# A DLRM tower on one core: ten features by one-hot matmul, two samples per dot-product matmul, gathers issued two at a time

## The chip, the core and the metric

The kernel runs on one core of a Trainium2 chip. The metric is the device time of one execution in microseconds (us). The engines are named as the profile names them: PE (TensorE, matmuls), PEld (its weight loads), DVE (VectorE), ACT (ScalarE), POOL (GpSimd, which issues the gathers), SP (SyncE, which issues the other transfers).

## The reference

2048 samples. Each has a dense vector of 128 numbers and 26 ids, each of which picks one row of 128 numbers from its own table. The tables have 1000, 1250, 12500 or 125000 rows.

```python
e = jnp.stack([tbl_0[ids[:, 0]], ..., tbl_25[ids[:, 25]]], axis=1)
combined = jnp.concatenate([dense_features[:, None, :], e], axis=1)        # 27 vectors of 128
interactions = jnp.einsum('bnd,bmd->bnm', combined, combined)
z = jnp.concatenate([dense_features, interactions[:, _TRIU_I, _TRIU_J]], axis=1)   # 351 pairs
h = jnp.concatenate([z, r_dense_features], axis=1)
h = jnp.maximum(h @ W_top1 + b_top1, 0.0)     # 607 -> 512
h = jnp.maximum(h @ W_top2 + b_top2, 0.0)     # 512 -> 256
y = h @ W_top3                                # 256 -> 1
```

## The kernel before

The batch is 16 tiles of 128 samples; a step handles two tiles (256 samples), so there are 8 steps, and the steady ones run in a hardware loop with two steps per iteration. Vector 0 is the dense one, vectors 1 to 26 the features.

**Fetching a feature.** The vectors come in two ways.
- Nineteen features per tile are gathered: POOL issues an indirect DMA for each (L322 in `gather_tile`), which brings 128 rows of 512 bytes, one per sample, into `rows[v % 2]`. The features are in five groups (3, 4, 4, 4 and 4 gathers; the first group also holds the dense vector). Ahead of group k of tile v POOL waits until PE has transposed group k of tile v-2, which frees that part of the buffer (L317). Nothing else holds a gather back, so POOL issues up to 19 in a row. PE then turns each vector with a transpose (L359) into `vec_ps`, and ACT and DVE by turns copy groups into `vecs` (L577).
- Seven features (`SPREAD`, all with tables of 1000 rows) are fetched by one-hot matmuls, called items. The table lies in SBUF as 125 partitions by 8 rows, split into `t_hi` and `t_lo`. PE copies a feature's ids onto all partitions (L388, `ids_ps`), DVE compares them with the row numbers in two halves (L726, `onehot`), PE multiplies (16 matmuls of 256 columns, L406, into `fetch_ps`), and ACT copies the result into `vecs` (L594). The items of a step fetch for the next step. There is one `fetch_ps`, so an item waits for the ACT copy of the one before.

**Dot products.** One matmul per sample (L381): the sample's 27 vectors against themselves, 128 per tile, in four quadrants of 32 samples. ACT copies the 27x27 products into `inter` (L630, 16 copies per tile), DVE merges those of a second place over them (L805, 16 per tile); then ACT and DVE split `inter` into `x_hi` and `x_lo` (L638, L815).

**Layers.** Layer 1 (L453, 60 matmuls of 256 columns per step), layer 2 (L469), layer 3 (L483), with the activations on ACT (L650, L656). They run for the step before the one being fetched.

**Order.** The order on PE, ACT and DVE is written by hand in each engine's `step`; PE's mixes items and layers between transposes and dot products, so that a tile's transposes come once per half step. POOL's order is plain: tile after tile, group after group. The tables for the items are loaded by SP at the start (seven of 512 KB), together with the weights.

## Time and profile of the kernel before

| | us |
|---|---|
| median of 3 runs | 721.52 (720.75 to 726.87) |
| span of the profiled execution | 724.9 |
| PE busy | 437.8 (60%) |
| PEld busy | 397.8 (55%) |
| POOL busy | 294.0 (41%) |
| DVE busy | 276.1 (38%) |
| ACT busy | 195.9 (27%) |
| moved by DMA | 28.01 MB, mean 39 GB/s |

The profiled execution is one of its own, 3.4 us above the median. Busy time is that in which an engine executes; what ended the idle time ahead of an instruction is called its releaser and is inferred from semaphores. "issue" means that nothing the profile shows was waited for; "remote" that the releaser was not found. Matmuls overlap in the pipeline, so the distance between their starts, not their own length, is what a row of them costs.

### The profile page before, as it was taken

Reading aid. Unit: us, or ns where it says so; the run is one execution under the profiler, and the core shown is the slowest. Engines: PE = TensorE matmul, PEld = TensorE weight load, DVE = VectorE, ACT = ScalarE, POOL = GpSimd, SP = SyncE. Lnnn points to the kernel's source line nnn. Section 1 sums busy time; section 2 is a strip of 40 time slices with the busy share of each in tenths; the row PEclk is TensorE's granted clock in tenths of the full one; section 3 lists DMA queues with packets and bytes.
Section 4 is the critical chain, followed back from the end, with each engine's and each line's share of the span. In section 5 each row is a group of like instructions: output and inputs, shape, how many; then the busy total and the mean of one; then the engine's idle time right before and its main releaser. Section 6 shows DMA issues by size and latency. Waiting matters only on the chain.

```text
span 724.9 us, 14518 instructions
## 1 busy us (share of the span) xinstructions
PE 437.8 (60%) x6057; PEld 397.8 (55%) x6057; DVE 276.1 (38%) x465; ACT 195.9 (27%) x443; POOL 294.0 (41%) x314
## 2 busy tenths in 40 slices
PE   4206365482955839276491856829376494946987
PEld 2206355471944729265391845728375383835886
DVE  4506444350523616234152433425134351532450
ACT  1104132140511314132240413204132141412552
POOL 7761716336072542706336072541706336171000
PEclk9957776697886959679596786959779596876999
DMA  5531211102020110201102020110201101020000
GB/s 128 166 107 37 52 60 45 30 23 52 2 57 18 32 44 15 56 7 42 34 22 53 3 55 20 37 37 12 55 12 45 29 21 48 13 58 13 3 2 1
DMA packets 19576, 28.01 MB, mean 39 GB/s; under 512 B 10691, under 2 KB 13267, under 8 KB 19518
## 3 DMA queue, kind: packets, MB, share of 16 engines
q0 software_dynamic: 9728, 19.94, 10.9%
q1 hardware_dynamic: 9790, 7.17, 3.4%
q8 instruction: 52, 0.85, 0.5%
q14 instruction: 6, 0.05, 0.0%
HBM read 27.08 MB, written 0.01 MB: 37 GB/s over the span
## 4 chain that ended last, share of the span: by engine, by line
PE 44%; another core or an unknown queue 27%; issue 16%; ACT 7%; DVE 3%; DMA 2%; SPq 1%; ACTq 0%; DVEq 0%
PE dots_ps L381 18%; PE fetch_ps L406 12%; PE h_ps L453 4%; PE vec_ps L359 4%; PE h_ps L469 3%; DMA vecs<-in_tbl 2%; ACT vecs L577 2%; ACT vecs L594 2%; DVE inter L805 2%; ACT inter L630 1%; PE ids_ps L388 1%; PE fetch_ps L453 1%; DVE vecs L577 1%; DVE onehot L726 1%
## 5 line engine op out<-in xcount | busy, mean ns | idle before, releaser
L322 POOL DMA_INDIRECT rows<-in_tbl,idx x304 | 291.5, 959 | 360.3 <-PE vec_ps L359 264.5
L406 PE MATMUL fetch_ps<-onehot,t_hi 125*128 125x256 f32 x448 | 134.5, 325 | 130.1 <-ACT vecs L594 108.3
L381 PE MATMUL dots_ps<-vecs 128*27 128x27 f32 x4096 | 136.0, 197 | 89.1 <-issue 56.8
L381 PEld LDWEIGHTS dots_ps<-vecs 128*27 128x27 f32 x4096 | 130.7, 114 | 98.9 <-issue 98.2
L726 DVE TENSOR_TENSOR onehot<-ids_ps,row_of 125x1024 fp32r<-125x1024 f32 x94 | 111.4, 1220 | 176.0 <-remote 134.7
L406 PEld LDWEIGHTS fetch_ps<-onehot,t_hi 125*128 125x128 f32 x448 | 97.8, 218 | 136.4 <-issue 129.2
L406 PE MATMUL fetch_ps<-onehot,t_lo 125*128 125x256 f32 x448 | 131.1, 321 | 7.6 <-issue 7.6
L406 PEld LDWEIGHTS fetch_ps<-onehot,t_lo 125*128 125x128 f32 x448 | 97.7, 218 | 11.5 <-issue 7.9
L805 DVE COPY_PREDICATED inter<-mask,dots_ps 27x128 f32<-27x128 int32 (+2 forms) x256 | 66.9, 261 | 97.1 <-ACT inter L630 90.8
L594 ACT COPY vecs<-fetch_ps 128x256 f32<-128x256 f32 x56 | 37.7, 673 | 223.4 <-remote 153.8
L630 ACT COPY inter<-dots_ps 27x128 f32<-27x128 f32 (+1 forms) x256 | 64.1, 250 | 74.3 <-PE dots_ps L381 65.4
L577 ACT COPY vecs<-vec_ps 128x512 f32<-128x512 f32 x40 | 48.0, 1199 | 103.4 <-remote 57.2
L577 DVE COPY vecs<-vec_ps 128x512 f32<-128x512 f32 x40 | 47.3, 1181 | 61.5 <-remote 50.8
L359 PE MATMUL vec_ps<-ident,rows 128*128 128x128 f32 x320 | 47.4, 280 | 6.3 <-ACT vecs L577 4.4
L359 PEld LDWEIGHTS vec_ps<-ident,rows 128*128 128x128 f32 x320 | 37.2, 143 | 11.2 <-issue 6.1
L453 PE MATMUL h_ps<-x_hi,w_hi 128*128 128x256 f32 x140 | 37.1, 296 | 0.5 <-ACT x_hi L638 0.5
L453 PE MATMUL h_ps<-x_hi,w_lo 128*128 128x256 f32 x140 | 36.3, 290 | 0.0
L726 DVE TENSOR_TENSOR onehot<-h_ps,row_of 125x1024 fp32r<-125x1024 f32 x16 | 19.5, 1227 | 42.9 <-remote 37.7
L483 PE MATMUL h_ps<-w_sb,h_sb 128*128 128x1 f32 x48 | 11.2, 355 | 39.0 <-ACT h_sb L656 20.6
L483 PEld LDWEIGHTS h_ps<-w_sb,h_sb 128*128 128x128 f32 x48 | 10.7, 327 | 40.2 <-ACT h_sb L656 21.3
L469 PE MATMUL h_ps<-h_sb,w_sb 128*128 128x256 f32 x128 | 32.5, 381 | 0.1
L453 PEld LDWEIGHTS h_ps<-x_hi,w_hi 128*128 128x128 f32 x140 | 26.6, 190 | 1.3 <-issue 0.7
(65 smaller groups left out, 232.5 us busy)
## 6 DMA issues: line engine op xcount, KB each, us to landing
rows<-in_tbl,idx POOLq DMA_INDIRECT x304
vecs<-in_tbl SPq DMA_DIRECT2D x6, 500.0 KB
rows<-in_r_dense_features SPq DMA_DIRECT2D x16, 64.0 KB
h_sb<-in_W_top_laid SPq DMA_DIRECT2D x2, 512.0 KB
w_sb<-in_W_top SPq DMA_DIRECT2D x1, 512.0 KB
w_sb<-in_tbl SPq DMA_DIRECT2D x1, 500.0 KB
idx<-in_ids SPq DMA_DIRECT2D x16, 13.0 KB
w_dense<-in_W_top SPq DMA_DIRECT2D x1, 256.0 KB
```

Of the source, the lines that this page charges most:

```text
L322: nc.gpsimd.indirect_dma_start(out=rows[v % 2][:, s, :], out_offset=None, in_=tables[f - 1][:, :], in_offset=bass.IndirectOffsetOnAxis(ap= ...
L359: last = pe.transpose(vec_ps[kk % 2][:, n * P:(n + 1) * P], rows[u][:, s, :], ident[:])
L381: last = pe.matmul(dots_ps[q * 32:q * 32 + N, n // HALF, o:o + N], vs[:, b, :], vs[:, b, :], start=True, stop=True)
L406: last = pe.matmul(fetch_ps[:, 0:R], part[0:KP, k, h * KH + t, :], onehot[buf][h][0:KP, t, :], start=(h == 0 and t == 0 and part is t_hi), ...
L453: last = pe.matmul(bank[:, m, :], w[:, jj, c0:c0 + P], x[:, jj, :], start=(at == 0), stop=(at == 3 * (JG + 1) - 1))
L469: last = pe.matmul(h2_ps[:, m, :], w2_sb[:, k, m * P:(m + 1) * P], h1_sb[:, k, :], start=(n % M1 == 0), stop=(n % M1 == M1 - 1))
L483: last = pe.matmul(y[:, t:t + 1], h2_sb[:, k, t * P:(t + 1) * P], w3_sb[:, k:k + 1], start=(k == 0), stop=(k == M2 - 1))
L577: copy(vecs[v // 2][:, v % 2, :, a:a + n].rearrange("p b f -> p f b"), vec_ps[kk % 2][:, 0:n * P].rearrange("p (f b) -> p f b", f=n)).then ...
L594: nc.scalar.copy(vecs[slot][:, :, :, NR + k], fetch_ps[:, 0:R].rearrange("p (t b) -> p t b", t=2)).then_inc(fetched, 1)
L630: nc.scalar.copy(inter_of(q, g, 0, count[g]), products_of(q, g * JG, count[g])).then_inc(inter_by_act, 1)
L726: dve.tensor_tensor(onehot[buf][h][0:KP], ids_at(m)[0:KP].rearrange("p (o r) -> p o r", o=1).to_broadcast([KP, KH, R]), row_of[0:KP, h * K ...
L805: dve.copy_predicated(inter_of(q, g, a, n), mask[g * 32:g * 32 + N, a:a + n].rearrange("p (j h s) -> p j h s", h=1, s=1).to_broadcast([N, ...
```

## The change

- Three more features (2 and 8, tables of 1250 rows, and 1, of 1000 rows) are fetched by items: ten items per step instead of seven. An item of a 1250-row table has 20 matmuls and compares ten rows per partition instead of eight. Sixteen features per tile are gathered, in groups of 2, 4, 4, 4 and 2.
- All gathers go out by two: before each pair POOL waits until the pair ahead of it has landed (`gathered`). Ahead of a tile's first pair it also waits until the whole of tile v-2 is transposed, where before each group had a wait of its own. The first pass over four tiles is written out ahead of the loop.
- Dot products: one matmul handles two neighbouring samples. Its stationary operand is 64 columns (2 samples of 27 vectors padded to 32), its moving one 54; the products of a sample with itself are two diagonal blocks of the result. `dots_ps` holds 64 samples, so a tile is two units with 32 matmuls each, and a unit waits until the one before is copied and merged. There are 32 product copies and 32 merges per tile, each of half the samples.
- An item's result goes to `found` by one contiguous copy, and `place` puts all ten into `vecs` with one copy per tile (128x128x10). `vecs` holds one step instead of two.
- The ids of the item features come transposed from memory; PE turns none. Each table is loaded in two transfers (112 and 13 partitions), 2 of 640 KB and 8 of 512 KB in all. Layer 1 runs as four parts in two banks (`mlp_ps`), layer 3 with the weights stationary, the result is written as rows. The orders of PE, ACT and DVE are written anew. The memory set aside for POOL's DMA descriptors is set to 2048.

The diff, cut:

```diff
-SPREAD = (5, 6, 9, 14, 18, 24, 26)
+SPREAD = (2, 8, 1, 5, 6, 9, 14, 18, 24, 26)
+AT_ONCE = 2
...
-    groups = [list(range(a, min(a + 4, NR))) for a in range(0, NR, 4)]
+    groups = [list(range(a, b)) for a, b in ((0, 3), (3, 7), (7, 11), (11, 15), (15, 17))]
...
+    KT = [tables[f - 1].shape[0] // KP for f in SPREAD]
...
-        vecs = [sb(f"vecs{s}", [P, 2, P, N]) for s in range(2)]
+        vecs = sb("vecs", [P, 2, P, NP])
+        found = sb("found", [P, X, R])
...
-        dots_ps = ps("dots_ps", [P, 2, 512])
+        dots_ps = ps("dots_ps", [P, QS, SLOT])
+        mlp_ps = [ps(f"mlp_ps{m}", [P, 512])[:, 0:R] for m in range(2)]
...
+            for n in range(X):
+                load_table(n)
+                if n < 2:
+                    load_dense(0, n)
+                    load_idx(0, n + 1)
+            load_idx(0, 3)
...
-            def gather_tile(i, v):
+            def gather_tile(i, v, first):
                 pool.wait_ge(idx_in[v], i * 16 + 16)
                 for k, group in enumerate(groups):
-                    pool.wait_ge(transposed, i * (4 * NG) + groups_of(v - 2) + k + 1)
+                    mine = [s for s in group if ORDER[s]]
+                    if k == 0:
+                        pool.wait_ge(transposed, i * (4 * NG) + groups_of(v - 1))
+                    if k or not (first and v == 0):
+                        if k:
+                            ii, vv, kk = i, v, k - 1
+                        elif v:
+                            ii, vv, kk = i, v - 1, NG - 1
+                        else:
+                            ii, vv, kk = i - 1, 3, NG - 1
+                        n = len([s for s in groups[kk] if ORDER[s]])
+                        pool.wait_ge(gathered[vv % 2][kk], ii * (32 * n) + (vv // 2 + 1) * 16 * n)
                     pool.sem_inc(groups_begun, 1)
-                    for s in group:
+                    landed = i * (32 * len(mine)) + v // 2 * (16 * len(mine))
+                    for n, s in enumerate(mine):
                         f = ORDER[s]
-                        if f:
-                            nc.gpsimd.indirect_dma_start(
-                                out=rows[v % 2][:, s, :], out_offset=None, in_=tables[f - 1][:, :],
-                                in_offset=bass.IndirectOffsetOnAxis(ap=idx[v][:, f - 1:f].bitcast(U32), axis=0),
-                            ).then_inc(gathered[v % 2][k], 16)
-            pool.iota(row_of_i[:], pattern=[[1, KT]], base=0, channel_multiplier=KT).then_inc(rows_counted, 1)
+                        if n and n % AT_ONCE == 0:
+                            pool.wait_ge(gathered[v % 2][k], landed + 16 * n)
+                            pool.sem_inc(gathers_resumed, 1)
+                        nc.gpsimd.indirect_dma_start(
+                            out=rows[v % 2][:, s, :], out_offset=None, in_=tables[f - 1][:, :],
+                            in_offset=bass.IndirectOffsetOnAxis(ap=idx[v][:, f - 1:f].bitcast(U32), axis=0),
+                        ).then_inc(gathered[v % 2][k], 16)
...
-            with pool.Fori(0, PASSES) as i:
+            for v in range(4):
+                gather_tile(0, v, True)
+            with pool.Fori(0, PASSES - 1) as i:
                 for v in range(4):
-                    gather_tile(i, v)
+                    gather_tile(i + 1, v, False)
...
-            def dots(i, v):
...
-                for b in range(P):
-                    q, n = b // QS, b % QS
-                    o = (n % HALF) * N
-                    last = pe.matmul(dots_ps[q * 32:q * 32 + N, n // HALF, o:o + N], vs[:, b, :],
-                                     vs[:, b, :], start=True, stop=True)
-                    if n == QS - 1:
-                        last.then_inc(dots_done, 1)
...
+            def dots(i, v, u, spread=None):
+                vs = vecs[:, v % 2]
+                first = static(i) and i == 0 and v == 0
+                if u == 0:
+                    pe.wait_ge(vecs_by_act, i * 12 + (v + 1) * 3 + 1)
+                    pe.wait_ge(vecs_by_dve, i * 8 + (v + 1) * 2 + 1)
+                    pe.wait_ge(placed, i * 4 + v + 1)
+                    if first:
+                        pe.wait_ge(pads_zero, 2)
+                if not (first and u == 0):
+                    pe.wait_ge(inter_by_act, i * (4 * NA) + v * NA + u * (1 + PER_UNIT))
+                    pe.wait_ge(inter_by_dve, i * (4 * ND) + v * ND + u * PER_UNIT)
+                for h in range(2):
+                    if h and spread:
+                        round_, k, m = spread
+                        pe.wait_ge(compared, m * 2)
+                    for n in range(QS):
+                        b = u * UNITS * 2 * QS + h * 2 * QS + n * 2
+                        last = pe.matmul(dots_ps[h * 64:h * 64 + 64, n, 0:PAIR],
+                                         vs[:, b:b + 2, :].rearrange("p b f -> p (b f)"), vs[:, b:b + 2, 0:N],
+                                         start=True, stop=True)
+                        if h and spread and n == 0:
+                            spread_ids(round_, k)
...
-                    spread_ids(i * 2 + r + 1, 0)
-                    def with_layer1(k):
-                        layer1(*prev, 0, shares(k, L1))
-                        if k == ITEM_AFTER[0]:
-                            fetch_items(i, r, IN_TILE)
-                    def with_layer2(k):
-                        layer2(*prev, shares(k, L2))
-                        if k == ITEM_AFTER[1]:
-                            fetch_items(i, r, IN_TILE_2)
-                    transpose_rows(i, v, after=with_layer1)
-                    fetch_items(i, r, BEFORE_DOTS)
-                    dots(i, v)
-                    layer1(*prev, 1)
-                    fetch_items(i, r, AFTER_LAYER1)
-                    transpose_rows(i, v + 1, after=with_layer2)
-                    fetch_items(i, r, AFTER_LAYER2)
-                    layer3(*prev)
-                    fetch_items(i, r, AFTER_LAYER3)
+                    transpose_rows(i, v, (0, 1))
+                    fetch_items(i, r, 0)
+                    transpose_rows(i, v, (2, 3, 4))
+                    layer1(*prev, 0)
                 else:
                     for k in range(X):
-                        spread_ids(0, k, k)
-                    fetch_first(range(EARLY))
-                    transpose_rows(i, v)
-                    fetch_first(range(EARLY, X - 1))
-                    for k in range(BANKED):
-                        spread_ids(1, k, X + k)
-                    fetch_first([X - 1])
-                    dots(i, v)
-                    fetch_items(i, r, [0, 1])
-                    transpose_rows(i, v + 1)
-                    fetch_items(i, r, range(2, X - 2))
-                dots(i, v + 1)
-                fetch_items(i, r, LAST if prev else [X - 2, X - 1])
+                        pe.wait_ge(lo_made, k + 1)
+                        if k == X - 1:
+                            pe.wait_ge(ids_cast, 2)
+                        fetch(k, k, k % 2, ((k + 1) // X, (k + 1) % X, k + 1))
+                        if k == X - 4:
+                            pe.wait_ge(ident_made, 1)
+                        if k >= X - 4:
+                            transpose_rows(i, v, (k - X + 4,))
+                    transpose_rows(i, v, (4,))
+                    fetch_items(i, r, 0)
+                dots(i, v, 0, spread_of(i, r, 2))
+                fetch_items(i, r, 1)
+                if prev:
+                    layer1(*prev, 1, 2)
+                else:
+                    transpose_rows(i, v + 1, (0, 1))
+                fetch_items(i, r, 2)
+                dots(i, v, 1)
+                if prev:
+                    transpose_rows(i, v + 1, (0, 1))
+                fetch_items(i, r, 3)
+                if prev:
+                    layer1(*prev, 3)
+                transpose_rows(i, v + 1, (2, 3, 4))
+                fetch_items(i, r, 4)
+                dots(i, v + 1, 0)
+                fetch_items(i, r, 5)
+                if prev:
+                    layer2(*prev, 0)
+                fetch_items(i, r, 6)
+                if prev:
+                    layer2(*prev, 1)
+                fetch_items(i, r, 7)
+                dots(i, v + 1, 1)
+                fetch_items(i, r, 8)
+                if prev:
+                    layer3(*prev)
+                fetch_items(i, r, 9)
...
-            def copy_fetched(slot, k, m):
+            def copy_fetched(k, m):
                 act.wait_ge(onehot_used, m * 2 + 2)
-                nc.scalar.copy(vecs[slot][:, :, :, NR + k],
-                               fetch_ps[:, 0:R].rearrange("p (t b) -> p t b", t=2)).then_inc(fetched, 1)
-            def copy_items(i, r, ks):
+                nc.scalar.copy(found[:, k, :], fetch_ps).then_inc(fetched, 1)
+            def copy_items(i, r, *ks):
                 for k in ks:
-                    copy_fetched((r + 1) % 2, k, item(i, r, k)[0])
+                    if k == 0:
+                        act.wait_ge(placed, i * 4 + r * 2 + 2)
+                    copy_fetched(k, item(i, r, k)[0])
+            def place(i, r, t):
+                if not (static(i) and i == 0 and r == 0):
+                    act.wait_ge(dots_done, i * (8 * UNITS) + r * (4 * UNITS) - (1 - t) * 2 * UNITS)
+                if t == 0:
+                    act.wait_ge(fetched, i * (2 * X) + (r + 1) * X)
+                nc.scalar.copy(vecs[:, t, :, NR:N],
+                               found[:, :, t * P:(t + 1) * P].rearrange("p k b -> p b k")).then_inc(placed, 1)
...
+    nc = bacc.Bacc("TRN2", target_bir_lowering=False, num_devices=1, dynamic_dma_scratch_size=2048)
...
+    given["ids_spread"] = np.ascontiguousarray(given["ids"][:, [f - 1 for f in SPREAD]].T)
```

Three places show how it moves instructions. On POOL, at the start of tile 0, before (`rows0` is the buffer of even tiles, `in_tbl_n` the table of feature n+1):

```order
L322 DMA rows0<-in_tbl_0,idx0 128x128 [waits transposed]
L322 DMA rows0<-in_tbl_1,idx0 128x128
L322 DMA rows0<-in_tbl_2,idx0 128x128
L317 REGISTER_ALU
L322 DMA rows0<-in_tbl_3,idx0 128x128 [waits transposed]
L322 DMA rows0<-in_tbl_6,idx0 128x128
L322 DMA rows0<-in_tbl_7,idx0 128x128
```

and in the changed kernel:

```order
L297 DMA rows0<-in_tbl_2,idx0 128x128 [waits idx_in0,transposed]
L297 DMA rows0<-in_tbl_3,idx0 128x128
L297 DMA rows0<-in_tbl_6,idx0 128x128 [waits gathered0_0]
L297 DMA rows0<-in_tbl_9,idx0 128x128
L297 DMA rows0<-in_tbl_10,idx0 128x128 [waits gathered0_1]
L297 DMA rows0<-in_tbl_11,idx0 128x128
L297 DMA rows0<-in_tbl_12,idx0 128x128 [waits gathered0_1]
```

The waits for transposes between the groups are gone, and every second gather waits for the landing of the two before it (`gathered0_k` is group k of the even tiles).

On PE, at the first tile's dot products in a step of the loop, before:

```order
L376 ISA [waits fetched,vecs_by_dve,vecs_by_act]
L377 ISA [waits inter_by_act]
L381 MATMUL dots_ps<-vecs 27x27 [waits inter_by_dve]
L381 MATMUL dots_ps<-vecs 27x27 x127
L448 ISA
L453 MATMUL h_ps<-x_hi,w_hi 128x256 [waits relu1_done]
```

and in the changed kernel:

```order
L348 ISA [waits placed]
L349 REGISTER_ALU [waits inter_by_act]
L357 MATMUL dots_ps<-vecs 64x54 [waits inter_by_dve]
L357 MATMUL dots_ps<-vecs 64x54 x15
L354 ISA
L357 MATMUL dots_ps<-vecs 64x54 [waits compared]
L365 MATMUL ids_ps<-ids_t,pick 128x256
L357 MATMUL dots_ps<-vecs 64x54 x15
L370 REGISTER_ALU
L380 MATMUL fetch_ps<-onehot_0,t_hi 128x256 [waits fetched,compared]
```

One block of 128 matmuls became two units of 32, with an item or more (and parts of the layers) between them, and the dots wait for `placed` instead of `fetched`.

On ACT, ahead of the first tile's products in a step of the loop, before:

```order
L593 ISA
L594 COPY vecs<-fetch_ps 128x256 [waits onehot_used]
L576 REGISTER_ALU
L577 COPY vecs<-vec_ps 128x4x128 [waits transposed]
L593 ISA
```

and in the changed kernel, from the loop's start:

```order
L545 ISA [waits dots_done]
L546 COPY vecs<-found 128x128x10 [waits fetched]
L511 REGISTER_ALU
L512 COPY vecs<-vec_ps 128x128x3 [waits transposed]
L543 REGISTER_ALU
L546 COPY vecs<-found 128x128x10 [waits dots_done]
L537 ISA
L530 ISA [waits placed]
L531 COPY found<-fetch_ps 128x256 [waits onehot_used]
```

The two placing copies stand around the first transposed group's copy, ahead of the step's first item copy.

## Rows read from the trace of the kernel before

**Rows 1.** The page: share of the chain that ended last, by engine

```profile
PE 44%; another core or an unknown queue 27%; issue 16%; ACT 7%; DVE 3%; DMA 2%; SPq 1%; ACTq 0%; DVEq 0%
```

**Rows 2.** Waits: engine, line <- releaser: us in total, times, longest us

```profile
POOL rows L322 <- PE vec_ps L359: 264.5, 20, 21.7
PE fetch_ps L406 <- ACT vecs L594: 108.3, 16, 26.5
ACT vecs L594 <- remote: 153.8, 17, 28.8
DVE onehot L726 <- remote: 172.4, 17, 17.4
```

**Rows 3.** Timeline of POOL: start us, us, instruction, [idle before <-releaser]

```profile
372.54 0.95 POOL L322 DMA_INDIRECT rows<-in_tbl,idx  x1 [17.53 <-PE vec_ps L359]
373.79 0.94 POOL L322 DMA_INDIRECT rows<-in_tbl,idx  x1 [0.30 <-issue]
...
395.05 0.94 POOL L322 DMA_INDIRECT rows<-in_tbl,idx  x1 [0.30 <-issue]
...
415.98 1.16 POOL L322 DMA_INDIRECT rows<-in_tbl,idx  x1 [19.98 <-PE vec_ps L359]
```

**Rows 4.** Windows: us, busy us of PE PEld DVE ACT POOL, PEclk, DMA share, GB/s

```profile
372.00:396.00 24.00, 11.45 (x72) 9.99 (x70) 8.72 (x8) 3.89 (x6) 17.97 (x19) 0.78 0.20 53
415.00:427.00 12.00, 10.41 (x81) 9.35 (x80) 7.78 (x7) 4.05 (x5) 8.39 (x9) 1.00 0.17 45
427.00:443.00 16.00, 2.25 (x19) 1.42 (x18) 0.00 (x0) 1.64 (x3) 9.79 (x11) 0.59 0.20 50
```

**Rows 5.** Timeline of PE and ACT in the burst of 372.54

```profile
371.13 1.04 PE L359 MATMUL vec_ps<-ident,rows 128*128 128x128 f32 x8
...
375.07 0.28 PE L406 MATMUL fetch_ps<-onehot,t_lo 125*128 125x256 f32 x1
...
381.30 0.28 PE L406 MATMUL fetch_ps<-onehot,t_lo 125*128 125x256 f32 x1
...
375.39 0.68 ACT L594 COPY vecs<-fetch_ps 128x256 f32<-128x256 f32 x1 [2.01 <-PE fetch_ps L406]
...
399.60 0.66 ACT L594 COPY vecs<-fetch_ps 128x256 f32<-128x256 f32 x1 [12.00 <-remote]
```

**Rows 6.** DMA page of 394 to 400 us, in 40 slices: GB/s

```profile
GB/s 0 246 191 0 0 0 0 0 0 164 191 27 55 0 0 0 0 27 273 109 28 0 0 0 0 0 0 0 0 0 0 0 0 0 0 0 0 0 0 0
```

**Rows 7.** Timeline of PE: back-to-back item matmuls, dots in a quiet stretch

```profile
370.05 0.28 PE L406 MATMUL fetch_ps<-onehot,t_lo 125*128 125x256 f32 x1
370.17 0.28 PE L406 MATMUL fetch_ps<-onehot,t_hi 125*128 125x256 f32 x1
...
404.82 7.44 PE L381 MATMUL dots_ps<-vecs 128*27 128x27 f32 x256
```

**Rows 8.** The page, part 5: line engine op xcount | busy, mean ns | idle before

```profile
L726 DVE TENSOR_TENSOR onehot<-ids_ps,row_of 125x1024 fp32r<-125x1024 f32 x94 | 111.4, 1220 | 176.0 <-remote 134.7
L805 DVE COPY_PREDICATED inter<-mask,dots_ps 27x128 f32<-27x128 int32 (+2 forms) x256 | 66.9, 261 | 97.1 <-ACT inter L630 90.8
L594 ACT COPY vecs<-fetch_ps 128x256 f32<-128x256 f32 x56 | 37.7, 673 | 223.4 <-remote 153.8
L577 ACT COPY vecs<-vec_ps 128x512 f32<-128x512 f32 x40 | 48.0, 1199 | 103.4 <-remote 57.2
```

**Rows 9.** Windows: one step of the loop (columns as in group 4)

```profile
352.00:440.00 88.00, 54.34 (x759) 49.67 (x758) 32.30 (x54) 23.25 (x54) 38.55 (x41) 0.77 0.13 33
```

**Rows 10.** Timelines of POOL and PE; DMA rate of 0 to 90 us in 40 slices

```profile
3.76 1.13 POOL L322 DMA_INDIRECT rows<-in_tbl,idx  x1 [0.53 <-issue]
...
654.05 0.95 POOL L322 DMA_INDIRECT rows<-in_tbl,idx  x1 [0.31 <-issue]
...
695.73 0.60 PE L359 MATMUL vec_ps<-ident,rows 128*128 128x128 f32 x4
...
GB/s 5 105 106 144 166 164 166 164 153 169 166 146 168 170 164 190 153 231 205 95 44 44 58 58 0 0 0 0 0 7 73 193 55 58 58 56 38 51 58 51
```

706 lines of the change are left out of this document (338 added, 368 removed).

## The prediction

> **What bounds the kernel now.** I began with the chain that ended last. PE holds 44% of it, but 27% goes to a releaser that the profile could not find and 16% to "issue" [rows 1]: more than 40% is work that was ready and yet did not go on. The waits say who stands still. POOL waits 264.5 us for PE's transposes, PE 108.3 us for ACT's copy of an item, and ACT and DVE 153.8 and 172.4 us for "remote" [rows 2]. So it is a ring: POOL waits for PE, PE for ACT and DVE, and these for nobody visible. The timeline closes it.
>
> POOL works in bursts, 19 gathers at 1.25 us each (0.95 busy, 0.30 between), and then idles 17.5 to 20 us [rows 3]. In the burst that begins at 372.54 the item matmuls that start last at 375.07 are copied from 375.39, at once. The next item's last matmul starts at 381.30, and ACT copies it at 399.60, 18 us late, though ACT had nothing else to do [rows 5]. The last gather of that burst starts at 395.05, and its data moves in the third cluster, 396.55 to 397.15 [rows 6]; 2.4 us later ACT wakes. PE itself slows down, too: it is busy 11.45 of the 24 us of the burst, and in the next one 10.41 of the first 12 us and 2.25 of the following 16 [rows 4]. So a long run of gathers holds back PE and the signals between the engines, not in its first three gathers but from then until it is over; and then POOL waits for the PE that it held back. A step takes 88 us, in which PE is busy 54.34 [rows 9].
>
> **The change, part by part.** *Pairs.* The second gather starts 1.25 us after the first [rows 3], its data is in 2.1 us after its own start [rows 3, 6], and I add 0.25 for the signal. From a transpose's signal to POOL's next gather it took about 0.8 us: the first group of the transposes that start at 371.13 is three of the eight, done about 371.7, and POOL starts at 372.54 [rows 3, 5]. A pair is 1.25 + 2.35 + 0.8 = 4.4 us; a tile has 8 pairs, 35.2 us, and all 16 tiles 563 us. This is dearer per gather (2.2 us for 1.25), but 256 are left of 304, and POOL gives up the idle time. Bounds of a pair: 4.1 (the wake-up in 0.5) and 4.9 (POOL's first gather after a wait takes 1.16 in place of 0.95 [rows 3], and the signal 0.3 more); each tenth is 13 us on the whole.
>
> *Does the hold vanish?* The row has it absent for a burst's first three gathers. Between a pair's landing and the next pair's first data lie 0.8 + 1.5 (start to data, 395.05 to 396.55) = 2.3 us without any gather's data under way, and no more than two are ever outstanding. I take it as gone, the lower bound. The upper bound is a hold as strong as in the bursts.
>
> *PE's work.* Item matmuls start 0.12 us apart [rows 7]; 168 for 112 in a step is 20.2 us for 13.4, so +6.8. Dots: 256 records in 7.44 us, 29 ns each [rows 7]; now 128 records per tile with twice the moving columns. Between 29 ns (3.7 us) and 58 ns (7.4 us) I take 50, so 6.4 us, 12.8 per step for 14.9: -2. Six fewer transposes take off about 0.8. PE has 51 us of its own work per step at full clock, 25.5 per tile, against 35.2 us of gathering: covered by 10 us. If that cover were gone, each us per tile would cost 16.
>
> *DVE and ACT.* Compares 1.22 us [rows 8], 16 of them plus 4 that are a quarter longer: 25.6 us per step. 64 merges of half the samples at about 0.21 (0.26 for the whole [rows 8]): 13.4; copies 4.7, split 1.6: 46 us of 70.4. ACT: 64 products at 0.22 are 14, ten item copies at 0.67 [rows 8] 6.7, two placings of 1280 elements at the rate of 512 in 1.2 us [rows 8] 6, the rest 8: 35 us. Both hidden. The placings stand ahead of the dots (6 us and two other copies, against 5 us of item, transposes and layer 1 on PE), which costs PE 3 or 4 us of its 10. The second unit of a tile waits for the first one's merges; between them in a step are items and layers of 6 us or more, which cover it, but not at the end of the kernel.
>
> *The start.* POOL's first gather starts at 3.76 [rows 10]; its set-up is a little longer, 4.5. The tables are 5.4 MB for 3.5. At the start some 165 GB/s are moved for 40 us [rows 10]; 5.4 MB, 1.8 MB of weights and the gathers keep this up until about 55 us, 10 pairs. A pair's 131 KB at half that rate takes 1.6 us instead of 0.6: +1.0 each, 10 us. Tile 2's gathers want the first tile transposed at 85; ahead of that PE has ten items, and even at twice the 2.4 us of their two compares [rows 8] these are 49 us behind the first table, which lands some 10 us in: covered.
>
> *The end.* Before, POOL was done at 655 and the last transposes began only at 695.73 [rows 10], 40 us of backlog; from there to the end of the span (724.9) it took 29.2. Now the last tile is transposed when it lands. Add 1 for that hop and 3 for the second unit: 33.
>
> Sum: 4.5 + 563.2 + 10 - 0.8 (no pair after the last) + 33 = **610** for the profiled execution, which was 724.9 before. That one was 3.4 above the median of 721.52, so the median should come to **607**.
>
> **The rivals.**
> *A, the pairs still hold PE partly.* Speaks for it: gathers are then under way half of all time, and the wake-up after a burst took 2.4 us, as long as the gap of 2.3. Let p be the share of its speed that PE keeps while POOL is gathering. A tile takes 35.2 + 25.5 - 35.2p where that is more than 35.2. At p = 0.65 it is 37.8, times 16 plus 46.7 for start and end: 652. Against it: PE goes on at 375, with three gathers issued.
>
> *B, the hold stays as it is, and the kernel is slower.* In the burst of 372 PE was busy 11.45 of 24 us, p = 0.48 [rows 4]: a tile takes 43.8, and the whole 748. It decides at p = 0.52, where a tile takes 42.4 and nothing is gained. For it: the pace of PE in these rows; against it: the first 10 us of a burst, where PE was busy 10.41 of 12.
>
> *C, gathers don't hold anybody.* Then PE's idle time has another cause, such as its own hops between engines, and remains, and what this change adds to PE is paid in full: 4 to 5 us per step, 8 steps, about +36, so 758 to 761. Against it: the copy 18 us late, and its wake-up right behind the last gather's data [rows 5, 6], in this burst and, with the same shape, in the others (17 waits of ACT with 153.8 us [rows 2]).
> The Trainium skill, "SBUF — State Buffer", section "Who interferes with whom", speaks for C: it says that PE and ACT never wait on anyone, and that a DMA never contends with a compute engine. By that rule the time would be C's 760; by the rows it is 607. It is a rule on ports, and the rows may show signals held back and not ports, which is why I give it little.
>
> *D, cheaper pairs.* If a landing is seen sooner and POOL wakes in 0.4, a pair is 3.95 us: 506 + 46.7 = 552.
>
> *E, no difference.* A hold near the break-even of B, 721.
>
> **How the numbers follow.** Forecast 0.60, with a range of its own of 580 to 650 (pairs of 4.2 to 4.65). A 0.12 (650 to 705), B 0.10, C 0.06, D 0.08 (545 to 580), E 0.04. Faster by over 1%: 0.60 + 0.12 + 0.08 = 0.80; within 1%, about what a measurement of this kernel can tell from no change: 0.04; slower: 0.16. The range leaves B, C and E out and so reaches from 560 to 705.
>
> **What would show it.** In the profile of the changed kernel: POOL's gathers in pairs 4.4 us apart, 35 us per tile, evenly, with POOL's idle time ended by DMA (landings) and next to nothing by PE. ACT's item copies would start within 0.5 us of the item's last matmul, and the "remote" waits of ACT and DVE would fall from 150 to 170 us to under 30. A step would take 70 us, PE busy 50 of it, idle for rows to land. I am wrong on the price if the pairs are evenly spaced at another distance. I am wrong on the hold if the copies stay late or POOL again waits 10 us for transposes (A, B); C shows if PE waits in short hops that the pairs don't change. If DVE's or ACT's waits in a ring with PE fill the step, the layout of the units is at fault, which I priced as hidden.

## The result, and the profile after

| | before | changed |
|---|---|---|
| median | 724.19 us (720.75 to 727.74, 4 runs) | 670.35 us (668.47 to 672.54, 4 runs) |
| span of the profiled execution | 724.9 us | 667.5 us |

The ratio is 0.9265 (95% interval 0.9214 to 0.9316): 7.4% faster. I had forecast 607 us, 16% faster. The direction and the bound were right, the size was half. Later groups of runs added something that the forecast hadn't thought of at all: in two of five groups the kernel *before* took 442 and 444 us in the median (below). All that is said of a gain holds for the other three groups and for these first measurements, where it took 718 to 724.

From the page of the changed kernel, the busy times and POOL's group (line engine op, count | busy, mean ns | idle before it), and the DMA issues (last number: median us from issue to landing):

```profile
PE 509.0 (76%) x4385; PEld 453.6 (68%) x4385; DVE 363.1 (54%) x760; ACT 249.5 (37%) x750; POOL 250.6 (38%) x267
...
L297 POOL DMA_INDIRECT rows<-in_tbl,idx x256 | 246.8, 964 | 375.4 <-DMA rows<-in_tbl,idx 301.5
...
rows<-in_tbl,idx POOLq DMA_INDIRECT x256, 2.5
```

Its waits (us in total, times, longest):

```profile
POOL rows L297 <- DMA rows<-in_tbl,idx: 301.5, 114, 8.8
ACT found L531 <- PE fetch_ps L380: 137.5, 62, 6.6
DVE onehot L687 <- PE ids_ps L365: 123.1, 47, 8.6
...
PE vec_ps L334 <- DMA rows<-in_tbl,idx: 96.0, 24, 8.7
```

Against [rows 2] everything has turned round. POOL no longer waits for PE's transposes (264.5 us before) but for its own landings, PE waits for rows to land, and of the "remote" waits of ACT and DVE (153.8 and 172.4 us before) 4.7 us are left, on ACT. Here is an item's end on PE and its copy on ACT, just as POOL starts the second gather of a pair, and one between two pairs (gathers at 217.19 and 220.63):

```profile
203.18 0.28 PE L380 MATMUL fetch_ps<-onehot,t_lo 125*128 125x256 f32 x1
203.18 0.94 POOL L297 DMA_INDIRECT rows<-in_tbl,idx  x1 [0.30 <-issue]
...
203.49 0.37 ACT L531 COPY found<-fetch_ps 128x256 f32<-128x256 f32 x1 [1.71 <-PE fetch_ps L380]
...
219.60 0.28 PE L380 MATMUL fetch_ps<-onehot,t_lo 125*128 125x256 f32 x1
...
219.91 0.37 ACT L531 COPY found<-fetch_ps 128x256 f32<-128x256 f32 x1 [0.80 <-PE fetch_ps L380]
```

The copy starts 0.31 us after the start of the item's last matmul in both, where [rows 5] had 18 us. The timeline of POOL, in the start and in the middle:

```profile
4.98 1.15 POOL L297 DMA_INDIRECT rows<-in_tbl,idx  x1 [0.18 <-issue]
...
16.16 0.94 POOL L297 DMA_INDIRECT rows<-in_tbl,idx  x1 [8.78 <-DMA rows<-in_tbl,idx]
...
25.62 1.56 POOL L297 DMA_INDIRECT rows<-in_tbl,idx  x1 [7.28 <-DMA rows<-in_tbl,idx]
...
33.86 0.94 POOL L297 DMA_INDIRECT rows<-in_tbl,idx  x1 [5.43 <-DMA rows<-in_tbl,idx]
...
38.46 0.94 POOL L297 DMA_INDIRECT rows<-in_tbl,idx  x1 [2.40 <-DMA rows<-in_tbl,idx]
...
206.68 0.94 POOL L297 DMA_INDIRECT rows<-in_tbl,idx  x1 [2.55 <-DMA rows<-in_tbl,idx]
207.92 0.94 POOL L297 DMA_INDIRECT rows<-in_tbl,idx  x1 [0.30 <-issue]
211.40 0.94 POOL L297 DMA_INDIRECT rows<-in_tbl,idx  x1 [2.53 <-issue]
```

A pair takes 4.72 us here (206.68 to 211.40), and the first three pairs 28.9 us together (4.98 to 33.86). Tile 1's gathers start at 57.63, tile 15's, 14 tiles on, at 591.74: 38.15 us per tile, 4.77 per pair. A step is 76.3 us. At the end:

```profile
591.74 0.94 POOL L297 DMA_INDIRECT rows<-in_tbl,idx  x1 [2.65 <-issue]
...
625.99 0.94 POOL L297 DMA_INDIRECT rows<-in_tbl,idx  x1 [0.30 <-issue]
628.56 0.69 PE L334 MATMUL vec_ps<-ident,rows 128*128 128x128 f32 x2 [3.60 <-DMA rows<-in_tbl,idx]
629.04 3.62 PE L423 MATMUL mlp_ps<-h_sb,w_sb 128*128 128x256 f32 x8
632.59 3.75 PE L357 MATMUL dots_ps<-vecs 128*64 128x54 f32 x64
635.70 3.78 DVE L745 COPY_PREDICATED inter<-mask,dots_ps 27x48 f32<-27x48 int32 x16 [10.00 <-ACT inter L571]
...
639.78 3.75 PE L357 MATMUL dots_ps<-vecs 128*64 128x54 f32 x64
...
648.59 0.55 PE L414 MATMUL mlp_ps<-x_hi,w_hi 128*128 128x256 f32 x1 [5.06 <-DVE x_lo L753]
```

### The profile page after: what moved, and what is told of

It is laid out like the page before. It is cut to its first block and busy times, and to the rows that moved or that the text cites. A ratio compares the mean times of both kernels' runs of the same rounds, so it can differ in the third digit from the quotient of the medians.

```text
span 667.5 us, 12112 instructions
## 1 busy us (share of the span) xinstructions
PE 509.0 (76%) x4385; PEld 453.6 (68%) x4385; DVE 363.1 (54%) x760; ACT 249.5 (37%) x750; POOL 250.6 (38%) x267
## 5 line engine op out<-in xcount | busy, mean ns | idle before, releaser
L297 POOL DMA_INDIRECT rows<-in_tbl,idx x256 | 246.8, 964 | 375.4 <-DMA rows<-in_tbl,idx 301.5
L687 DVE TENSOR_TENSOR onehot<-ids_ps,row_of 125x1024 fp32r<-125x1024 f32 (+1 forms) x162 | 200.5, 1274 | 127.8 <-PE ids_ps L365 123.1
L380 PE MATMUL fetch_ps<-onehot,t_hi 125*128 125x256 f32 x672 | 197.2, 320 | 30.6 <-DVE t_lo L710 24.1
L380 PE MATMUL fetch_ps<-onehot,t_lo 125*128 125x256 f32 x672 | 196.0, 319 | 0.0
L380 PEld LDWEIGHTS fetch_ps<-onehot,t_hi 125*128 125x128 f32 x672 | 143.9, 214 | 40.1 <-DVE t_lo L710 26.9
L745 DVE COPY_PREDICATED inter<-mask,dots_ps 27x64 f32<-27x64 int32 (+2 forms) x512 | 106.3, 208 | 92.8 <-ACT inter L571 78.1
L380 PEld LDWEIGHTS fetch_ps<-onehot,t_lo 125*128 125x128 f32 x672 | 143.5, 214 | 10.8 <-issue 3.8
L357 PE MATMUL dots_ps<-vecs 128*64 128x54 f32 x2048 | 136.1, 237 | 2.1 <-ACT vecs L512 2.0
L357 PEld LDWEIGHTS dots_ps<-vecs 128*64 128x64 f32 x2048 | 131.0, 151 | 9.1 <-issue 3.6
L571 ACT COPY inter<-dots_ps 27x64 f32<-27x64 f32 (+1 forms) x512 | 102.6, 200 | 86.9 <-PE dots_ps L357 70.9
```

The lines of the kernel that those rows point to most:

```text
L297: nc.gpsimd.indirect_dma_start(out=rows[v % 2][:, s, :], out_offset=None, in_=tables[f - 1][:, :], in_offset=bass.IndirectOffsetOnAxis(ap= ...
L357: last = pe.matmul(dots_ps[h * 64:h * 64 + 64, n, 0:PAIR], vs[:, b:b + 2, :].rearrange("p b f -> p (b f)"), vs[:, b:b + 2, 0:N], start=Tru ...
L380: last = pe.matmul(fetch_ps, part[0:KP, T0[k] + h * KH[k] + t, :], onehot[buf][h][0:KP, t, :], start=(h == 0 and t == 0 and part is t_hi), ...
L571: nc.scalar.copy(inter_of(u, q, g, 0, count[g]), products_of(q, g * JG, count[g])).then_inc(inter_by_act, 1)
L687: dve.tensor_tensor(onehot[buf][h][0:KP, 0:kh], ids_ps[0:KP].rearrange("p (o r) -> p o r", o=1).to_broadcast([KP, kh, R]), rows_at[0:KP, h ...
L745: dve.copy_predicated(inter_of(u, q, g, a, n), mask[g * 32:g * 32 + N, a:a + n].rearrange("p (j s) -> p j s", s=1).to_broadcast([N, n, QS] ...
```

## The experiments

By the hold I mean what the prediction describes: during a long run of gathers PE and the signals between the engines come late. My theory: the changed kernel is bound by the chain of landings, a round trip per pair, and the landing waits are what frees PE. The rivals: PE is still held partly and shares the bound (A), or gathers hold nobody (C).

The ratios below are to the kernel before, run beside each group on the same chip. A group is a set of kernels that were run together.

### First group: how many at a time

Kernel before in this group: 720.21 us.

**One at a time** (`AT_ONCE = 1`).

> The changed kernel with one gather at a time instead of two (AT_ONCE 1). In the trace of the changed kernel a gather's data is in 2.2 us after its start and POOL goes on 1.27 us later. Theory 1 (the chain of landings is all that bounds it): a gather costs 3.5 us, a tile 56, the kernel 56 x 16 plus the 56 us that start and end take = about 950 us. Theory 2 (PE, partly held back by the pairs, shares the bound): with one gather in flight PE is freer, so the time rises by much less than the chain, to 850 or below.

Measured: 940.16 us, ratio 1.305 (1.295 to 1.315). The chain predicts 950, so theory 1 holds: no second bound damped the rise. POOL waits 604.9 us for landings.

**A wait per group** (`AT_ONCE = 4`, rounds of 2, 4, 4, 4, 2).

> The changed kernel with AT_ONCE 4: POOL waits for a landing only ahead of each group, so the rounds of a tile are 2, 4, 4, 4 and 2 gathers. Theory 1 (chain of landings, and a hold only behind long bursts): 2 x 4.75 + 3 x (3 x 1.25 + 3.5) = 31 us per tile, which is about what PE is busy per tile (30.6), so 16 x 31 to 33 plus 56 = 555 to 585 us. Theory 2 (the hold grows with the gathers in flight): PE and the signals are late again from the fourth gather on, POOL waits for transposes, and the time is 650 us or more.

Measured: 603.85 us, ratio 0.837 (0.829 to 0.845). It lies 20 to 50 us above the chain's sum and below theory 2. In the windows view of it, PE is busy 0.87 of the time and has become part of the bound:

```profile
250.00:410.00 160.00, 138.76 (x1287) 123.56 (x1287) 102.91 (x212) 71.65 (x213) 71.94 (x77) 0.98 0.14 35
```

But the hold is not gone here, only shorter. ACT still waits for "remote" in its trace; the first two rows are from its waits, the others from its timeline, with the last gather of a round of four at 221.06:

```profile
ACT inter L571 <- remote: 39.4, 11, 4.8
ACT found L531 <- remote: 35.1, 11, 3.9
...
220.04 0.28 PE L380 MATMUL fetch_ps<-onehot,t_lo 125*128 125x256 f32 x1
221.06 0.95 POOL L297 DMA_INDIRECT rows<-in_tbl,idx  x1 [0.30 <-issue]
223.03 0.37 ACT L531 COPY found<-fetch_ps 128x256 f32<-128x256 f32 x1 [3.87 <-remote]
224.38 0.95 POOL L297 DMA_INDIRECT rows<-in_tbl,idx  x1 [2.38 <-DMA rows<-in_tbl,idx]
```

The item's last matmul starts at 220.04, and its copy starts 3.0 us later, 1.97 us after the last gather of the round. Of ACT's 24 waits of this kind in the run, 22 end 1.96 to 2.19 us after the start of the last gather of a round of four, which is about when that gather's data is in (2.1 us after its start [rows 6]). A signal due early in a round passes: the next item's last matmul starts at 225.93, with two gathers of the next round issued, and is copied at 226.25. One due late in a round is seen when the round is over. How much of the 20 to 50 us this costs, and how much PE's own work, isn't separated.

**One burst per tile.** The descriptor memory is a little larger, too, to hold 16 gathers.

```diff
-AT_ONCE = 2
+AT_ONCE = 4
...
-                    if k or not (first and v == 0):
+                    if k == 0 and not (first and v == 0):
...
-dynamic_dma_scratch_size=2048
+dynamic_dma_scratch_size=3072
```

> The changed kernel with the landing waits left out but for one per tile: the 16 gathers of a tile go out in one burst of 19 us. If the hold in long bursts is real and PE keeps 0.48 of its pace in it, a tile takes 22.2 x 0.52 + 30.6 = 42 us and the kernel about 730 us, with waits of ACT and DVE for no visible releaser as in the kernel before. If gathers hold nobody, PE bounds it at 31 us per tile: about 550 us.

Measured: 811.99 us, ratio 1.127 (1.118 to 1.136). The hold is back in full, even above my 730. The same kernel was run once more in the fourth group, and its trace is shown here:

> The changed kernel with one burst of 16 gathers per tile, which took 812 us beside a kernel before of 720. With the hold it should repeat 800 to 820; without it, PE's own work bounds it at about 31 us per tile: 550 to 570 us.

Measured: 810.91 us, 1.116 (1.097 to 1.135). Its waits, and the window of one burst (us, busy us of PE, PEld, DVE, ACT, POOL, then PEclk):

```profile
POOL rows L297 <- PE vec_ps L334: 392.9, 14, 34.3
ACT inter L571 <- remote: 253.4, 27, 14.0
...
318.40:338.20 19.80, 7.27 (x78) 6.28 (x77) 3.98 (x10) 2.27 (x10) 15.08 (x16) 0.74 0.19 55
```

PE keeps 0.37 of its time in the burst, less than the 0.48 of [rows 4]. Without the landing waits, the changed kernel is slower than the old one. In this group and the fourth they carry the whole gain.

**The gathers alone.** Nothing but 256 gathers, by two.

> Nothing but the 256 gathers by two, waiting for landings as in the changed kernel; no other engine works, and the result is zeros. If the 4.7 to 4.8 us of a pair are its own round trip, it takes the same here; if traffic and signals of the other engines lengthen it, it falls to the 4.4 that I had forecast, or at most to the shortest seen in the changed kernel, 4.5 us.

Measured: 600.03 us (one execution). Its timeline:

```profile
203.44 0.94 POOL L53 DMA_INDIRECT rows<-in_tbl,idx  x1 [2.35 <-DMA rows<-in_tbl,idx]
204.69 0.94 POOL L53 DMA_INDIRECT rows<-in_tbl,idx  x1 [0.31 <-issue]
208.01 0.94 POOL L53 DMA_INDIRECT rows<-in_tbl,idx  x1 [2.38 <-DMA rows<-in_tbl,idx]
209.26 0.94 POOL L53 DMA_INDIRECT rows<-in_tbl,idx  x1 [0.30 <-issue]
212.52 0.94 POOL L53 DMA_INDIRECT rows<-in_tbl,idx  x1 [2.32 <-DMA rows<-in_tbl,idx]
```

4.57 and 4.51 us for these pairs; over all tiles (starts at 41.4 to 560.0, 14 tiles) 37.0 us per tile, 4.63 per pair. Neither end of what I expected: most of the excess over my 4.4 is the round trip's own (0.23), and 0.14 comes with the other engines and transfers beside it.

### Second group: the landing waits in the kernel before, and the window

Kernel before in this group: 718.5 us.

**A sliding window of two** in the changed kernel. Gather n waits for n-2; odd and even gathers of a group count on semaphores of their own.

```diff
+                        if j >= 2 or not (first and v == 0):
...
+                            pool.wait_ge(gathered[vv % 2][kk][jj % 2],
+                                         ii * (32 * m) + vv // 2 * (16 * m) + 16 * (jj // 2 + 1))
+                            pool.sem_inc(gathers_resumed, 1)
```

> The changed kernel with a sliding window: gather n waits for the landing of gather n-2, so two are nearly always in flight (own semaphores for odd and even gathers). Theory 1 (only the number in flight brings the hold on): a gather's round trip is 3.4 us as in the run with one at a time, two in flight give 1.7 us each, 27 us per tile, so PE bounds the kernel at 31 to 33 us per tile: 560 to 600 us. Theory 2 (it is the quiet gap of about 2.9 us between the data of two pairs that frees PE): without the gap the hold returns with two in flight, and the time is 650 us or more, with ACT and DVE waiting for no visible releaser.

Measured: 570.15 us, ratio 0.796 (0.792 to 0.800), inside theory 1's 560 to 600. PE is busy 184.52 of 200 us, at a granted clock of 0.99:

```profile
200.00:400.00 200.00, 184.52 (x1797) 167.12 (x1795) 137.29 (x297) 97.35 (x301) 98.36 (x104) 0.99 0.15 39
```

So the quiet gap of 2.9 us between two pairs' data is not needed, and of the "remote" waits a single one of 1.5 us is left. This version beats both kernels where the kernel before takes 720.

**The kernel before with a landing wait per group**, nothing else.

```diff
+                    if k or v:
+                        vv, kk = (v, k - 1) if k else (v - 1, NG - 1)
+                        n = len([s for s in groups[kk] if ORDER[s]])
+                        pool.wait_ge(gathered[vv % 2][kk], i * (32 * n) + (vv // 2 + 1) * 16 * n)
```

> The kernel before, with one addition: ahead of each group POOL waits until the group before it has landed, so at most 4 of its 19 gathers per tile are in flight (rounds of 3, 4, 4, 4, 4). If the landing waits alone bring the gain: 6.0 + 4 x 7.2 = 35 us per tile, against 27 us of work for PE, so 16 x 35 + 50 = 610 to 640 us. If the gain of the change needs its other parts (fewer gathers, dots of two samples), PE stays late and the time is 690 us or more.

Measured: 609.6 us, ratio 0.846 (0.841 to 0.851), the lower edge of the expected range. Four lines in the old kernel bring twice the gain of the whole change, and about as much as the changed kernel with four at a time (0.837, 0.829 to 0.845, in the first group). Where both go by four, the new dots, the three moved features and the placing of vectors add nothing that these runs can tell. The hold is shorter here as well, not gone: in the profiled execution, which took 629.29 us, ACT waits 96.0 us in 20 waits for "remote", none longer than 5.8 us (28.8 in [rows 2]).

**The kernel before by two** (the same, with a wait after every second gather of a group as well).

> The kernel before with its gathers by two until landed (10 rounds per tile, since groups of 3 and 4 give 2, 1, 2, 2 and so on), nothing else changed. By the chain of landings 9 x 4.75 + 3.4 = 46 us per tile, so 16 x 46 + 45 = about 785 us, slower than before, with no wait of POOL for PE left. If something else in the pairs made the gain, it is faster than before.

Measured: 768.11 us, ratio 1.070 (1.063 to 1.077). This is what the fewer gathers are for: with pairs, the ten rounds that 19 gathers per tile need here cost more than the hold did, and the eight rounds of 16 gathers cost less. The change needs its ten items because it gathers by two.

**Whole tables** (one transfer per table).

> The changed kernel with each table in one transfer of 125 partitions instead of two of 112 and 13. In the changed kernel the first three pairs took 28.9 us instead of 14.3, while 205 to 251 GB/s were moved; before, with whole tables, it was some 165. If the gathers only queue behind the tables' bytes, the load lasts longer and each pair in it is delayed less, and the sum stays: the second tile's gathers start at 57 us as before, give or take 4, and the time is the same. If the split transfers hold the gathers back in particular, the second tile starts by 50 us and the time falls by 7 us or more.

Measured: 680.51 us, ratio 0.948 (0.942 to 0.954). Now six pairs are slow instead of three: 4.98, 12.61, 20.48, 27.62, 34.95, 43.88, 51.91 are their starts, 46.9 us for six, where the split tables give 42.6. Tile 1 starts at 61.5 instead of 57.6 (55.8 when the changed kernel was run again in the fourth group). So the split is not what holds the gathers back, against theory 2. But the sum does not quite stay either, as theory 1 had it: tile 1 starts 4 to 6 us later, and each later tile takes 38.8 us instead of 38.15, for which I have no cause.

### Third group: where the kernel before took 444 us

Kernel before in this group: 443.81 us (441.79 to 446.15, 7 runs), word for word the same program. Ratios here say little on the change. They say that the time it is compared with isn't fixed.

**The window of two in the kernel before.**

> The kernel before with a sliding window of two gathers and nothing else: gather n waits for the landing of n-2, in addition to the waits for transposes. 19 gathers at 1.75 us are 33 us per tile, above PE's 27 us of work, so 16 x 33 + 50 = about 580 us. Theory 1 (the way in which gathers are issued is all that the time hangs on): within 3% of the changed kernel with the same window (570). Theory 2 (the three features moved to matmuls and the dots of two samples carry a part of the gain): 610 us or more.

Measured: 586.62 us, 1.322 (1.315 to 1.330) of 443.81. The landings pace it: POOL waits 192.2 us for them, and nobody waits for "remote".

**Windows of three and of four in the changed kernel.**

> The changed kernel with a sliding window of three: gather n waits for the landing of n-3. A round trip of 3.4 us over three is less than the 1.25 us that POOL needs, so POOL issues without a pause while landings are seen in time. If the pace of the gathers brings the hold on, PE falls behind and the time is well above the window of two, 620 us or more; if it is the number in flight beyond two or three, it stays at about 570 us, bound by PE.

> The same with a window of four. In a burst the data of a gather is in 2.1 us after its start, so a window of four hardly ever has to wait by the data alone. If the pace brings the hold on, 700 to 810 us, close to the run with one burst per tile (812). If waits for landings as such prevent the hold, about 570 us.

Measured: 560.4 and 561.18 us, 1.263 and 1.265 of 443.81. Both fit the case without a hold of their expectations, but beside a kernel before of 444 they don't test it.

**A pause without landing waits.** The kernel with one burst per tile, two memsets ahead of each gather.

> The kernel with one burst of 16 gathers per tile (812 us), and two short memsets of POOL ahead of every gather, each waited for: a pause of about 0.5 us, so that gathers follow each other at 1.75 us as in the window of two, with no wait for a landing inside the tile. If the pace alone matters, the hold is gone and the time is 570 to 620 us. If it is the wait for landings that frees PE, it is still above 750 us.

Measured: 691.88 us, 1.560 of 443.81. POOL's own pace, 2.35 to 2.5 us per gather instead of the 1.75 I had meant, makes 40.2 us per tile and sets the time. The experiment missed its aim.

### Fourth and fifth group: is it a chance of the group?

**Both kernels once more, unchanged.**

> The kernel before, word for word, with a profile. In the last group of runs it took 444 us, in the two groups ahead of that 716 to 726. Theory 1 (the hold of PE in bursts is a state of the chip or of how the programs were loaded, which comes and goes): its time is near either 720 or 444; where it is 444, matmul signals arrive within 0.02 us even late in a burst of gathers, POOL waits for PE's own work only, and a step takes about 48 us. Theory 2 (the 444 us are a fault of that group): 720 us, always.

> The changed kernel, word for word, beside it. Its time is set by the landings of the pairs in either state, so it should be 665 to 675 us in both: 7% faster than before where before takes 720, and 50% slower where before takes 444. If pairs are themselves delayed by what holds PE, it falls below 650 in the second state.

Fourth group, kernel before 723.76: the same program once more 726.37 us (1.003, 0.997 to 1.009), the changed kernel 665.99 us (0.916, 0.900 to 0.933). Both theories allow the 726, so this run doesn't part them; the fifth group does, where the kernel before took 442 again. The changed kernel came within its forecast.

**The window of four, the window of two in the kernel before, and the pause, once more.**

> The sliding window of four once more, since its first run (561 us) fell in the group in which the kernel before took 444 us and no burst held PE. Beside a kernel before of 720: if a window of four is as good as none, the hold shows and it takes 700 to 812 us; if waiting for a landing four gathers back is enough to prevent it, 560 to 600 us. Beside one of 444: 560 us again, which tells nothing new.

> The kernel before with the sliding window of two, once more for the same reason (first run 587 us beside 444). The window keeps POOL at 1.77 us per gather in either state, 33 us per tile, so 580 to 600 us beside a kernel before of 720, if the window prevents the hold. If it doesn't in this kernel, 640 us or more.

> The pause of POOL ahead of every gather without landing waits inside the tile, once more (first run 690 us beside 444; POOL took 2.35 us per gather, so its own pace set the time). Beside a kernel before of 720: if the pace matters and not the wait for landings, 690 us again, with PE on time; if only landing waits prevent the hold, 750 us or more and PE late.

Fifth group, kernel before 442.04: 561.39, 589.39 and 692.12 us (1.268, 1.331 and 1.563), all as in the third group and again beside a kernel before of 442. So these three kernels tell nothing on whether windows of three or four, the window of two in the old kernel, or a pause would free PE where it is held. What they show is a burst that holds nobody. The window view of the window of four, one whole burst of 16 gathers at 1.25 us:

```profile
293.20:312.90 19.70, 19.29 (x204) 17.45 (x203) 13.16 (x26) 7.28 (x30) 15.06 (x16) 1.00 0.22 55
```

PE is busy 19.29 of 19.70 us, against 7.27 of 19.80 in the burst of the fourth group, at the same rate of gathers (55 GB/s in both). Inside it, POOL and ACT:

```profile
309.38 0.95 POOL L292 DMA_INDIRECT rows<-in_tbl,idx  x1 [0.30 <-DMA rows<-in_tbl,idx]
...
309.43 0.37 ACT L527 COPY found<-fetch_ps 128x256 f32<-128x256 f32 x1 [1.83 <-PE fetch_ps L376]
```

The landing waits cannot be what frees PE here: inside the burst POOL goes on after its usual 0.30 us each time, and the kernel before has none and took 442. No engine waits for "remote" in the traces of these two groups.

**What stays open.** Whether the hold is there was the same for all executions of the kernel before within a group: there in three groups and in the first measurements, absent in two. The two shared three kernels (window of four, window of two in the old kernel, pause), but were made on two different chips, one of which had shown the hold in the second group. It may be something that goes with what is loaded or was run beside, or chance. I have not found the cause, neither of the hold nor of its absence, and no trace of the kernel before at 442 us was taken.

## Why the prediction was right or wrong

**Bound and mechanism: right where the hold is present.** The signs I had named came: pairs evenly spaced, POOL's idle time ended by landings (301.5 us), copies on time, 4.7 us of "remote". The bursts (812 us) and the old kernel with waits (610 us) show by experiment that the long burst is the cause of the waits in [rows 2], and that waits for landings shorten them. Whether it must be a landing that POOL waits for, or a pause of the same length would do, no run shows, since the one with a pause missed its aim. Rival A, whose 652 was the nearest rival to the result, is not what happened: PE was not the bound. The time rises with the round trips alone when one gather goes at a time (940), and PE idles for landings for 96 us. That the result lies in A's range of 650 to 705 is a coincidence of the price of a pair.

Two readings of the rows were too sharp. "Though ACT had nothing else to do" is not so: in the 18 us it ran one activation, which came late itself, and its idle time ahead of the copy is 12.00 us.

```profile
386.76 0.84 ACT L656 ACTIVATE h_sb<-h_ps,b_sb 128x256 f32<-128x256 f32 x2 [5.93 <-remote]
```

And "I take it as gone" is right for the changed kernel only nearly: three waits of ACT, 4.7 us in all, end 1.6 to 1.7 us after the second gather of a pair, and in the kernel before by two there are 13, of 33.6 us. So the hold can begin with two gathers, earlier than I read it, and a short round ends it before it costs much.

**The size: wrong, in three terms.** My sum was 610 for the profiled execution, which came to 667.5.

| term | forecast | measured | difference |
|---|---|---|---|
| until tile 1's first gather | 47.7 (4.5 + 35.2 + 8) | 57.6 | +9.9 |
| from there to the last landing, some 628.4 | 529.2 (120 x 4.4 + 2 - 0.8) | 570.8 | +41.6 |
| end | 33 | 39.1 | +6.1 |

- *The pair, 4.4 us.* It is 4.77. This is the step that failed: "I add 0.25 for the signal" and, behind it, POOL's waking, for which I took the 0.8 us of a transpose's signal. A landing takes 2.5 us from the issue (the page, median), not 2.35, and POOL starts some 0.8 to 1.0 later. Alone on the chip a pair takes 4.63. I had its bounds at 4.1 and 4.9 and took a value near the lower one, although every tenth is 13 us: an error of 8% in one term, repeated 120 times behind tile 1's start, was nearly three quarters of the miss.
- *The start.* I had 10 us for pairs during the table loads, at +1.0 for each of ten. It was +14.6 for the first three and about nothing afterwards, 6.6 more than the 8 us I had up to tile 1. Another 3 of the 9.9 are again the price of a pair, eight times. The tables came at 205 to 251 GB/s, not 165, and a gather beside them took far longer than the double time I gave it.
- *The end.* The last transposes start at 628.56 and layer 1 at 648.59, 20.0 us; before, 12.3 (695.73 [rows 10] to 708.07, the row below, of the kernel before). The second unit's dots start 7.2 us after the first one's (632.59, 639.78), when these are copied and merged (at 639.48). I had named that and priced it at 3; from the first dots to layer 1 it is 16.0 us for 10.4, so 5.6. What I had at nothing is PE's clock. PE now idles for rows up to the end, and the work behind the last rows starts at a granted clock (PEclk) of 0.50:

```profile
708.07 0.36 PE L453 MATMUL fetch_ps<-x_hi,w_hi 128*128 128x256 f32 x1 [1.57 <-ACT x_hi L638]
```

Windows of the changed kernel, and one of the kernel before (columns as in [rows 4]):

```profile
615.00:629.00 14.00, 2.22 (x10) 1.42 (x9) 0.71 (x1) 0.71 (x1) 5.66 (x6) 0.50 0.10 28
629.00:632.50 3.50, 3.50 (x10) 2.37 (x8) 0.00 (x0) 0.59 (x1) 0.00 (x0) 0.50 0.00 0
643.60:648.50 4.90, 0.00 (x0) 0.00 (x0) 3.49 (x14) 2.38 (x10) 0.00 (x0) 0.77 0.00 2
648.50:653.00 4.50, 4.41 (x21) 4.44 (x22) 0.00 (x0) 0.47 (x1) 0.00 (x0) 0.50 0.00 0
```

```profile
708.00:712.00 4.00, 3.93 (x34) 3.96 (x34) 0.68 (x1) 0.68 (x2) 0.00 (x0) 1.00 0.01 4
```

After 14 us with PE busy for 2.22, the granted clock is 0.50 (1.2 GHz), and the eight layer-2 matmuls ahead of the dots take 3.62 us. After the idle time of 643.60 to 648.50 it is 0.50 again for 4.5 us of layer 1, which before ran at 1.00 (2.4 GHz). From the start of layer 1 to the end of the span it took 18.9 us for 16.8 before, about 2 us more.

**The covered parts.** PE's dots were priced wrongly: 64 records take 3.75 us, 58 ns each, the upper bound, so dots of two samples save nothing on PE (15 us per step, as before). Where PE is the bound, a step of the changed layout takes 59.3 us (tile starts 267.56 and 326.90 in the window of four, granted clock 1.00), of which PE is busy 55.7, not the 51 that I had; the prediction doesn't show from which rows its 51 was summed. With pairs this was hidden under 76 us, as forecast; with a window of two or more it is most of what counts.

**Rival C.** I gave it 0.06, on the ground of "the copy 18 us late". Its premise is that gathers hold nobody, and in two groups of five the runs show just that. Its other half, that PE's idle time then has another cause and remains, none shows: where nobody is held, the kernel before takes 442 us, so C's time of 758 to 761 belongs to no group. In the other three the rows speak against C, as I said. The changed kernel was not run where the kernel before takes 442. Its pairs would take no less there: with a window of two a gather takes 1.76 us in those groups (33.4 us per tile of 19, kernel before) and 1.72 where the hold is present (changed kernel, 214.18 to 248.51 for 20). So it would come to some 665 again, slower than before by half. That is an inference.

The Trainium skill, "SBUF — State Buffer", section "Who interferes with whom", has PE and ACT never waiting on anyone. It is a rule on ports, and whether the hold has to do with ports no run tells. A burst in one group of runs agrees with it (PE 19.29 of 19.70 us busy), a burst in another does not (7.27 of 19.80), and it is the measurement that decides for each.

**The landing waits as such.** That 19 gathers per tile could be spaced by four instead of two, so that the rest of the change was not needed, did not occur to me. I had the price of a round of four in hand: 3 x 1.25 + 3.15 (1.25 between gathers, 2.35 + 0.8 to the next round).

## What to carry to other kernels

Where engines idle behind a signal that is already due, look at what POOL is doing, and try the smallest edit first: a wait for a landing every few gathers. Price a round trip from issue to landing to the next issue by a kernel that does nothing else, before it is multiplied by a hundred. And run the unchanged kernel beside every comparison: here it took 720 us in some groups and 442 in others, and a change that wins by 7% against the one would, as inferred above, lose against the other.

## What the runs showed of the hardware that I had not expected

- The same program took 713 to 733 us or 442 to 446 us, the one or the other throughout a group of runs; the mean granted clock was 0.76 to 0.81 in the first case and 0.95 to 0.98 in the second.
- Where the hold is present, a burst of 16 gathers leaves PE 0.37 of its time; with rounds of 4 or a window of 2 it is busy 0.87 and 0.92. In rounds of 4, a signal that falls due late in a round is seen 2.0 to 2.2 us after the round's last gather has started. The number of gathers with data outstanding does not explain the hold by itself, since the last gather of a burst, too, has its data in 2.1 us after its start [rows 6].
- While tables come in at 205 to 251 GB/s, the second gather of a pair is followed by the next pair 9.7, 8.2 and 6.4 us after its start, instead of 3.3 to 3.5.
- A matmul with 64 stationary and 54 moving columns of f32 takes two records of 58 ns (3.75 us for 64), one with 27 and 27 two of 29 ns (7.44 us for 256 [rows 7]). Which of the two counts of columns sets the price, no run parts.
